# Side products of the band stages move from the rounds to the places in front of rounds one and two, into two banks, with VectorE as their copier

## The chip, the cores and the metric

The kernel runs on one core of one Trainium2 chip. The metric is the device time of one execution in microseconds (us), the median of three timed runs. Engines: TensorE (PE in the rows; its weight loads PEld), VectorE (DVE), ScalarE (ACT), GpSimd (POOL) and SyncE (SP, whose queue issues DMA).

## The reference

Two layers on x of 4 sequences of 512 positions with 128 features, each an attention part and a part with experts. The first layer's attention is the one at stake: each position t looks at a window of the 64 positions that end with it, in 16 heads.

```python
disp = (x @ W_disp).reshape(B, T, nh, bd).transpose(0, 2, 1, 3)       # 16 heads of 16
val = (x @ W_val).reshape(B, T, nh, hs).transpose(0, 2, 1, 3)         # 16 heads of 8
strain = disp_win - disp[:, :, :, None, :]                            # 64 neighbours of each t
bond_act = gelu(strain @ W_strain + rel_emb @ W_pos)
bond_logits = (bond_act @ W_bond)[..., 0]
damage_act = gelu(strain @ W_dmg + b_dmg)
damage = sigmoid((damage_act @ W_dmg_out)[..., 0] + b_dmg_out[0])
logits = where(cmask, bond_logits - 10.0 * damage, -inf)
weights = softmax(logits, axis=-1)
out = einsum('bntd,bntde->bnte', weights, val_win)                    # then @ W_cproj
```

The first layer's experts (16, four chosen for each position, with gate weights `route`) are added beside it: `acc = acc + r[..., None] * y`, and y holds a bias row of each expert, so that the biases together are the product of `route` with the 16 bias rows. The second layer is another attention and eight experts of which two are chosen.

## The kernel before, in words

Each engine has a program of its own, written out by hand, and signals (semaphores) tie them together. Between the stages all engines meet at a barrier.

The windowed attention is done for two groups of eight heads, `g` = 0 and 1. For each group there is first a long loop over the 64 neighbours, which leaves the logits in `Z`, and then a *band stage*, the one that the change touches. Stage one (g = 0) and stage two (g = 1) run the same code:

- TensorE's `weigh(k)` transposes the logits of one quarter (128 positions) into PSUM, VectorE takes the maximum and subtracts it (L832, L836), ScalarE takes the exponential (L872), four times.
- SyncE writes each quarter's weights to a DRAM tensor `band`, and SyncE and GpSimd read them back skewed into `wide` (L799), so that the windows become bands of a matrix. TensorE's first wait for such rows is `d_band_in0`.
- Then come four *rounds*, k = 0 to 3 (round one to four below). `turn(k)` transposes the round's 32 blocks in eight groups of four (L958) into four PSUM banks in turn. ScalarE copies the even groups to `wtT` (L898), VectorE the odd ones (L844), and a group waits until the copy of the group four before it is done. `values(k)` makes the value products of a round (L945), ScalarE copies them (L889). `gather(k)` forms denominators (L976) and numerators (L984) in the bank `summed(k)`, which is `WB[:, 3]` or `ZT[:, 8:12]` in turn, and VectorE's `divide(k)` takes the reciprocal and multiplies (L849, L851).
- `side(i)`, i = 0 to 7, stands twice in each round: behind `turn(k)` and behind `gather(k)`. It has nothing to do with the bands. In stage one side(i) is one product for the next loop: a part of `AD` for the group g = 1, L928, copied by ScalarE (L878). In stage two the sides with even i are four transposes of `route` (L935), copied by ScalarE to 16 partitions of `w1T` (L881), and the odd ones the four products with the experts' bias rows (L937), which VectorE adds to `ACC` (L856). All of them use the bank `WB[:, 2]`, so each waits until the one before is copied.

Behind stage one the next loop starts, behind stage two the second layer (L1177 is its first product). A stage ends when its last engine is done.

## Time and profile before

| | us |
|---|---|
| median of three timed runs | 1243.27 |
| lowest, highest | 1239.11, 1246.47 |
| profiled execution | 1248.83 |
| its span | 1247.1 |
| TensorE busy (share of the span) | 1033.0 (83%) |
| VectorE busy | 966.8 (78%) |
| ScalarE busy | 822.9 (66%) |
| GpSimd busy | 165.9 (13%) |

The span runs from the first to the last instruction; the time of the execution is a little longer. Busy shares are means over the whole program. A matmul of fp32 operands stands as two records in the profile and a transpose as one, each with a weight load of its own.

### The profile page before, as it was taken

What the parts mean: (1) busy time and instruction counts of PE and PEld (TensorE: products, weight loads), DVE (VectorE), ACT (ScalarE), POOL (GpSimd) and SP (SyncE); (2) the same over time, 40 slices, a digit from 0 to 9 for tenths busy, and PEclk for the clock granted to TensorE, in tenths of its full rate; (3) what the DMA queues carried; (4) which work ended last, traced back from release to release, by engine and by line L of the source; (5) the groups of instructions that cost most, each with busy time, mean ns of one, the idle gap of its engine ahead of it and who ended that gap; (6) DMA issues with size and microseconds to landing.
All of it is one profiled execution on the core that took longest, in us unless ns stands there. A gap on an engine that the chain in (4) does not pass through costs nothing. (4 is left out here: it accounts for less than half of the span.)

```text
span 1247.1 us, 23038 instructions
## 1 busy us (share of the span) xinstructions
PE 1033.0 (83%) x9629; PEld 533.1 (43%) x9629; DVE 966.8 (78%) x1221; ACT 822.9 (66%) x886; POOL 165.9 (13%) x257
## 2 busy tenths in 40 slices
PE   1679899998848499888899759898669999989887
PEld 1323333333447333333333358733315565556532
DVE  6699999999763799999999734558767467576746
ACT  0779999999762589999999652243146646565564
POOL 4100000000140100000000320313740000000072
PEclk9889999999979799999999968688569989989988
DMA  7310000000075200000000093000123423432221
GB/s 249 113 23 1 2 1 1 2 1 2 1 198 139 52 2 1 2 2 1 1 1 2 1 278 61 21 1 1 58 77 87 117 85 102 127 89 81 79 60 40
DMA packets 71750, 67.39 MB, mean 54 GB/s; under 512 B 6148, under 2 KB 63200, under 8 KB 71648
## 3 DMA queue, kind: packets, MB, share of 16 engines
q1 hardware_dynamic: 67808, 55.51, 15.8%
q0 software_dynamic: 3840, 10.43, 3.2%
q8 instruction: 76, 1.25, 0.4%
q14 instruction: 26, 0.21, 0.1%
HBM read 41.80 MB, written 20.97 MB: 50 GB/s over the span
## 5 line engine op out<-in xcount | busy, mean ns | idle before, releaser
L538 DVE SCALAR_TENSOR_TENSOR ring<-AD,PT 128x1808 f32<-128x1808 f32 (+15 forms) x128 | 284.0, 2219 | 4.0 <-POOLq L520 3.2
L683 PE MATMUL LG<-ring,lred 128*32 128x456 f32 (+15 forms) x2048 | 232.0, 572 | 1.3 <-ACT ring L635 1.3
L1841 DVE TENSOR_REDUCE MX<-SS 128x2 f32<-128x1024 f32 x128 | 155.6, 1219 | 67.0 <-PE SS L1583 66.7
L1771 ACT ACTIVATE EX<-SS 128x1024 f32<-128x1024 f32 x128 | 131.1, 1028 | 111.0 <-PE SS L1583 110.2
L625 ACT ACTIVATE ring<-ring 128x3616 f32<-128x3616 f32 (+15 forms) x50 | 169.9, 3398 | 3.7 <-DVE ring L538 3.7
L705 PE MATMUL SD<-DS,eyes 96*32 96x456 bf16 (+15 forms) x2496 | 156.7, 370 | 9.5 <-ACT ring L630 7.4
L633 ACT ACTIVATE ring<-ring 128x1824 f32<-128x1824 f32 (+15 forms) x78 | 141.0, 1807 | 0.0
L705 PEld LDWEIGHTS SD<-DS,eyes 96*32 96x32 bf16 x2496 | 57.8, 96 | 152.9 <-ACT ring L630 57.6
L538 DVE SCALAR_TENSOR_TENSOR ring<-AD,bdmg 128x1808 f32<-128x1808 f32 (+15 forms) x50 | 110.6, 2212 | 0.0
L718 PE MATMUL PY<-w2T,xg 128*128 128x128 f32 x512 | 74.1, 288 | 35.3 <-DVE xg L563 35.3
L683 PEld LDWEIGHTS LG<-ring,lred 128*32 128x32 f32 x2048 | 59.3, 110 | 99.3 <-issue 76.9
L1583 PE MATMUL SS<-KS,QS 32*128 32x512 f32 x256 | 72.5, 562 | 34.9 <-DVE MX L1841 32.3
L712 PE MATMUL PH<-tT,w1s 128*128 128x512 f32 x128 | 73.6, 658 | 30.3 <-DVE xg L558 23.4
L630 ACT ACTIVATE ring<-SD,bdmg 128x912 f32<-128x912 f32 (+15 forms) x78 | 82.8, 1062 | 22.2 <-PE SD L705 20.3
L718 PEld LDWEIGHTS PY<-w2T,xg 128*128 128x128 f32 x512 | 61.9, 191 | 70.0 <-DVE xg L563 55.5
L635 ACT ACTIVATE ring<-SD,bdmg 128x912 f32<-128x912 f32 (+15 forms) x78 | 82.6, 1059 | 1.4 <-PE SD L705 0.6
L570 DVE SCALAR_TENSOR_TENSOR ACC<-PY,route,ACC 128x128 f32<-128x128 f32 x256 | 71.6, 341 | 9.4 <-PE PY L718 9.4
L1603 PE MATMUL PW<-EX,VA 128*32 128x512 f32 x512 | 75.5, 668 | 0.1
L525 POOL COPY w1s<-w1T 128x128 f32<-128x128 f32 x16 | 12.6, 788 | 461.6 <-PE PH L712 461.6
L1583 PE MATMUL SS<-QS,KS 32*128 32x512 f32 x256 | 69.5, 543 | 5.3 <-ACT EX L1771 2.7
L1748 ACT ACTIVATE HB<-PHh,b1c 128x128 f32<-128x128 f32 x156 | 44.5, 368 | 31.0 <-PE PHh L1535 30.4
L1583 PEld LDWEIGHTS SS<-KS,QS 32*128 32x128 f32 x256 | 26.9, 204 | 85.4 <-DVE MX L1841 57.6
(338 smaller groups left out, 1500.8 us busy)
## 6 DMA issues: line engine op xcount, KB each, us to landing
w1s<-in_L_ffn_W SPq DMA_DIRECT2D x39, 256.0 KB, 3.0
w2s<-in_L_ffn_W SPq DMA_DIRECT2D x39, 256.0 KB, 3.0
band<-zs SPq DMA_DIRECT2D x8, 1024.0 KB, 8.8
wide<-band POOLq DMA_DIRECT2D x16, 380.0 KB, 8.9
wide<-band SPq DMA_DIRECT2D x16, 380.0 KB, 11.0
band<-Z SPq DMA_DIRECT2D x4, 1024.0 KB, 8.9
xs<-Z SPq DMA_DIRECT2D x4, 640.0 KB, 8.8
xl<-xs SPq DMA_DIRECT2D x10, 256.0 KB, 2.9
```

The lines of the kernel that those rows point to most:

```text
L538: return v.scalar_tensor_tensor(out=ring[:, slot, s, :, t0:T], in0=AD[:, s, :, j + t0:j + T], scalar=extra, in1=AD[:, s, :, PAD + t0:PAD + T],
L625: act.activation(tiles, tiles, ACT.Gelu).then_inc(gelu_done, 1)
L630: act.activation(ring[:, slot, 1, 0:2, t0:T], SD[:, :, t0:T], ACT.Gelu, bias=bdmg[:, 0:1]).then_inc(sd_taken, 1)
L633: act.activation(tiles, tiles, ACT.Gelu)
L635: act.activation(ring[:, slot, 1, 2:4, t0:T], SD[:, :, t0:T], ACT.Gelu, bias=bdmg[:, 0:1]).then_inc(gelu_done, 1)
L683: mm = pe.matmul(LG[32 * b:32 * b + 32, par, s, t0:T], lred[:, s, n % 4, :], ring[:, slot, s, b, t0:T], start=(n % 4 == 0), stop=(n % 4 == 3))
L705: mm = pe.matmul(SD[32 * q:32 * q + 32, i, t0:T], eyes[0:96, sign, :], DS[0:96, q, 2 * half + i, at:at + T - t0], start=(sign == 0), stop= ...
L718: mm = pe.matmul(PY[:, i, :], xg[:, c % 2, P * i:P * i + P], w2T[:, bass.ds(HG * g + it, 1), :].rearrange("p o c -> p (o c)"), start=True, ...
L1583: mm = pe.matmul(bank[:, n, :], rows[r:r + 32, b % 2, q, P * t:P * t + P], cols[r:r + 32, b % 2, q, :], start=True, stop=True)
L1603: mm = pe.matmul(PN[32 * hh:32 * hh + 32, :], VA[:, b % 2, t, 4 * q + hh, :], EX[:, q % 2, hh, t, :], start=(t == 0), stop=(t == NT - 1))
L1771: act.activation(EX[:, Q % 2, hh:hh + 2, t, :], SS[:, slot, :, :], ACT.Exp, scale=SCALE1).then_inc(freed[slot], 1)
L1841: v.tensor_reduce(MX[:, t, p // 2, hh:hh + 2], SS[:, slot, :, :], AX.X, ALU.max).then_inc(freed[slot], 1)
```

## The change

The four PSUM banks of transposes and the bank `WB[:, 3]` stay as they are. The side products now use `WB[:, 2]` and `ZT[:, 8:12]` in turn, and VectorE takes all of them out. They no longer stand in each round but at two places: five (stage one) or six (stage two) behind the four `weigh` and the first `values`, in front of round one, and three or two in front of round two. `gather(1)`, which sums into `ZT[:, 8:12]`, waits until all sides are copied. In stage two their order is other: two sets of transposes of `route`, then the two sets of products that use them, and so on, each to its own place in `w1T`.

TensorE in stage one, before, from the first value products (L945) over round one to the first transposes of round two. `wad` is the weight of a side product, `wide` the rows read back, `lones` and `vp` the operands of the sums:

```order
-L945 MATMUL ZT<-wval,xnT 128x64 x8
-L958 MATMUL WB<-ident,wide 128x128 x8
-L958 MATMUL ZT<-ident,wide 128x128 x8
-L958 MATMUL WB<-ident,wide 128x128 x8
-L958 MATMUL ZT<-ident,wide 128x128 x8
-L928 MATMUL WB<-xnT,wad 128x512
-L945 MATMUL ZT<-wval,xnT 128x64 x8
-L976 MATMUL WB<-wtT,lones 32x128 x32
-L984 MATMUL WB<-wtT,vp 32x64 x64
-L928 MATMUL WB<-xnT,wad 128x512
```

and now, where L956 are the values, L937 a side product, L969 the transposes of `wide`, L991 and L999 the sums:

```order
+L956 MATMUL ZT<-wval,xnT 128x64 x8
+L937 MATMUL WB<-xnT,wad 128x512
+L937 MATMUL ZT<-xnT,wad 128x512
+L937 MATMUL WB<-xnT,wad 128x512
+L937 MATMUL ZT<-xnT,wad 128x512
+L937 MATMUL WB<-xnT,wad 128x512
+L969 MATMUL WB<-ident,wide 128x128 x8
+L969 MATMUL ZT<-ident,wide 128x128 x8
+L969 MATMUL WB<-ident,wide 128x128 x8
+L969 MATMUL ZT<-ident,wide 128x128 x8
+L956 MATMUL ZT<-wval,xnT 128x64 x8
+L991 MATMUL WB<-wtT,lones 32x128 x32
```

One side product stood behind round one's transposes and one behind its sums. Now five stand in front of the transposes, and three more behind the sums, in front of the next round's transposes.

TensorE in stage two, before, the same place; L935 are transposes of `route`, L937 the products with the bias rows `b2r`:

```order
-L945 MATMUL ZT<-wval,xnT 128x64 x8
-L958 MATMUL WB<-ident,wide 128x128 x8
-L958 MATMUL ZT<-ident,wide 128x128 x8
-L958 MATMUL WB<-ident,wide 128x128 x8
-L958 MATMUL ZT<-ident,wide 128x128 x8
-L935 MATMUL WB<-ident,route 16x128 x4
-L945 MATMUL ZT<-wval,xnT 128x64 x8
-L976 MATMUL WB<-wtT,lones 32x128 x32
-L984 MATMUL WB<-wtT,vp 32x64 x64
-L937 MATMUL WB<-b2r,w1T 128x128 x4
```

and now, from behind the value products; L948 are the transposes of `route`, L946 the products:

```order
+L948 MATMUL WB<-ident,route 16x128 x4
+L948 MATMUL ZT<-ident,route 16x128 x4
+L946 MATMUL WB<-b2r,w1T 128x128 x4
+L946 MATMUL ZT<-b2r,w1T 128x128 x4
+L948 MATMUL WB<-ident,route 16x128 x4
+L948 MATMUL ZT<-ident,route 16x128 x4
+L969 MATMUL WB<-ident,wide 128x128 x8
+L969 MATMUL ZT<-ident,wide 128x128 x8
+L969 MATMUL WB<-ident,wide 128x128 x8
+L969 MATMUL ZT<-ident,wide 128x128 x8
+L956 MATMUL ZT<-wval,xnT 128x64 x8
+L991 MATMUL WB<-wtT,lones 32x128 x32
```

Four sets of transposes and two of products stand in front of round one.

VectorE in stage one, before, from the division behind round one (L849, L851) through its copies of round two (L844):

```order
-L849 RECIPROCAL Z<-WB 128x256
-L851 TENSOR_TENSOR attT<-WB,Z 128x2x128
-L844 COPY wtT<-WB 128x512
-L844 COPY wtT<-ZT 128x512
-L844 COPY wtT<-WB 128x512
-L844 COPY wtT<-ZT 128x512
```

and now, where L855 and L857 are the division, L863 the copy of a side product and L850 the copies of transposes:

```order
+L855 RECIPROCAL Z<-WB 128x256
+L857 TENSOR_TENSOR attT<-WB,Z 128x2x128
+L863 COPY AD<-ZT 128x512
+L863 COPY AD<-WB 128x512
+L863 COPY AD<-ZT 128x512
+L850 COPY wtT<-WB 128x512
+L850 COPY wtT<-ZT 128x512
+L850 COPY wtT<-WB 128x512
+L850 COPY wtT<-ZT 128x512
```

Three copies of side products stand between the division and the copies of round two.

```diff
--- before.py
+++ after.py
@@ -763,7 +763,7 @@
         with ExitStack() as sm:
             vp = sb(f"vp{g}", [P, 2, 8, HG, 32], F32, sm)
             zs = sb(f"zs{g}", [P, 2, NG, WIN, 4], F32, sm)
-            rtT = w1T[0:E0, 0:NT, :]
+            SIDES = ([0, 1, 2, 3, 4], [5, 6, 7]) if g < G - 1 else ([0, 1, 2, 3, 4, 5], [6, 7])
             wide = sb(f"wide{g}", [P, WIDE, NG, P, 4], F32, sm)
             wtT = sb(f"wtT{g}", [P, 32, P], F32, sm)
             diffs = [wtT[:, 16 * n:16 * n + 16, :].rearrange("p a t -> p (a t)").rearrange("p (n q j) -> p n q j", n=32, j=4) for n in range(2)]
@@ -783,6 +783,12 @@
 
             def turned(i):
                 return banks[i % 4]
+
+            def side_bank(i):
+                return ZT[:, 8:12, :] if i % 2 else WB[:, 2]
+
+            def pair_of(i):
+                return 2 * (i // 4) + i % 2, i % 4 >= 2
 
             def summed(k):
                 return ZT[:, 8:12, :] if k % 2 else WB[:, 3]
@@ -850,18 +856,30 @@
                     v.wait_ge(rc_ready, m + 1)
                     v.tensor_tensor(attT[:, g, :, P * ti:P * ti + P], summed(k)[:, 2:4, :], rc, ALU.mult).then_inc(att_ready, 1)
 
-                def bias(i):
-                    v.wait_ge(side_pe, 2 * i + 2)
-                    a = ACC[:, NT * i:NT * i + NT, :]
-                    v.tensor_tensor(a, a, WB[:, 2], ALU.add).then_inc(side_sb, 1)
+                def side(i):
+                    bank = side_bank(i)
+                    if g < G - 1:
+                        v.wait_ge(ad_pe, 8 + i + 1)
+                        v.tensor_copy(AD[:, i // 4, i % 4, PAD:PAD + T], bank.rearrange("p n t -> p (n t)")).then_inc(ad_sb, 1)
+                        return
+                    p, product = pair_of(i)
+                    v.wait_ge(side_pe, i + 1)
+                    if product:
+                        a = ACC[:, NT * p:NT * p + NT, :]
+                        v.tensor_tensor(a, a, bank, ALU.add).then_inc(side_sb, 1)
+                    else:
+                        v.tensor_copy(w1T[0:E0, NT * p:NT * p + NT, :], bank[0:E0]).then_inc(side_sb, 1)
 
                 for k in range(NT):
                     weigh(k)
+                for i in SIDES[0]:
+                    side(i)
                 for k in range(NT):
+                    if k == 1:
+                        for i in SIDES[1]:
+                            side(i)
                     turn(k)
                     divide(k)
-                    if g == G - 1:
-                        bias(k)
 
             @block.scalar
             def _(act):
@@ -871,14 +889,6 @@
                         act.wait_ge(d_out[k - 2], 16 * (g + 1))
                     act.activation(zs[:, k % 2].rearrange("p g s n -> p g n s"), diffs[k % 2].rearrange("p (g n) q j -> p g n (q j)", n=4), ACT.Exp
                                    ).then_inc(ex_ready, 1)
-
-                def side(i):
-                    if g < G - 1:
-                        act.wait_ge(ad_pe, 8 + i + 1)
-                        act.copy(AD[:, i // 4, i % 4, PAD:PAD + T], WB[:, 2].rearrange("p n t -> p (n t)")).then_inc(ad_sb, 1)
-                    elif i % 2 == 0:
-                        act.wait_ge(side_pe, i + 1)
-                        act.copy(rtT, WB[0:E0, 2]).then_inc(side_sb, 1)
 
                 def values(k):
                     m, par = M0 + k, k % 2
@@ -905,10 +915,8 @@
                 values(0)
                 for k in range(NT):
                     turn(k)
-                    side(2 * k)
                     if k + 1 < NT:
                         values(k + 1)
-                    side(2 * k + 1)
 
             @block.tensor
             def _(pe):
@@ -923,18 +931,21 @@
                     mm.then_inc(zt_ready, 1)
 
                 def side(i):
+                    bank = side_bank(i)
                     if g < G - 1:
-                        pe.wait_ge(ad_sb, 8 + i)
-                        pe.matmul(WB[:, 2].rearrange("p n t -> p (n t)"), wad[:, 1, i // 4, :], xnT[:, i % 4, PAD:PAD + T],
+                        pe.wait_ge(ad_sb, 8 + max(i - 1, 0))
+                        pe.matmul(bank.rearrange("p n t -> p (n t)"), wad[:, 1, i // 4, :], xnT[:, i % 4, PAD:PAD + T],
                                   start=True, stop=True).then_inc(ad_pe, 1)
                         return
-                    pe.wait_ge(side_sb, i)
+                    p, product = pair_of(i)
+                    if i >= 2:
+                        pe.wait_ge(side_sb, i - 1)
                     for n in range(NT):
-                        t = NT * (i // 2) + n
-                        if i % 2 == 0:
-                            mm = pe.transpose(WB[0:E0, 2, n, :], route[:, t, :], ident[:])
+                        t = NT * p + n
+                        if product:
+                            mm = pe.matmul(bank[:, n, :], w1T[0:E0, t, :], b2r[:], start=True, stop=True)
                         else:
-                            mm = pe.matmul(WB[:, 2, n, :], rtT[:, n, :], b2r[:], start=True, stop=True)
+                            mm = pe.transpose(bank[0:E0, n, :], route[:, t, :], ident[:])
                     mm.then_inc(side_pe, 1)
 
                 def values(k):
@@ -965,6 +976,10 @@
                     pe.wait_ge(vw_sb, m + 1)
                     if k >= 2:
                         pe.wait_ge(att_ready, m - 1)
+                    if k == 1 and g < G - 1:
+                        pe.wait_ge(ad_sb, 16)
+                    if k == 1 and g == G - 1:
+                        pe.wait_ge(side_sb, 8)
                     acc = summed(k)
 
 
@@ -991,13 +1006,16 @@
                 pe.wait_ge(zs_ready, M0 + 3)
                 values(0)
                 pe.wait_ge(zs_ready, M0 + NT)
+                for i in SIDES[0]:
+                    side(i)
                 for k in range(NT):
+                    if k == 1:
+                        for i in SIDES[1]:
+                            side(i)
                     turn(k)
-                    side(2 * k)
                     if k + 1 < NT:
                         values(k + 1)
                     gather(k)
-                    side(2 * k + 1)
 
 
 def second_layer(nc, t_in, out, l1, sb, psum, sem, ident, ACC, nhalf, stats, mv, rstd, carried):
```

## Rows read from the trace of the kernel before

**Rows 1.** Timeline of TensorE, stage one: start us, us, engine line operation tile, count, idle before

```profile
366.56 1.96 PE L958 MATMUL WB<-ident,wide 128*128 128x128 f32 x8 [9.67 <-DMA wide<-band]
...
371.96 1.02 PE L928 MATMUL WB<-xnT,wad 128*128 128x512 f32 x2
372.83 1.89 PE L945 MATMUL ZT<-wval,xnT 128*128 128x64 f32 x16
...
380.47 1.49 PE L984 MATMUL WB<-wtT,vp 128*32 128x64 f32 x44 [2.65 <-issue]
381.89 2.03 PE L928 MATMUL WB<-xnT,wad 128*128 128x512 f32 x2
383.76 1.12 PE L958 MATMUL WB<-ident,wide 128*128 128x128 f32 x8
...
387.60 1.02 PE L928 MATMUL WB<-xnT,wad 128*128 128x512 f32 x2
...
394.09 0.69 PE L984 MATMUL ZT<-wtT,vp 128*32 128x64 f32 x33 [0.52 <-issue]
394.71 1.13 PE L928 MATMUL WB<-xnT,wad 128*128 128x512 f32 x2
395.68 1.12 PE L958 MATMUL WB<-ident,wide 128*128 128x128 f32 x8
...
411.76 1.02 PE L928 MATMUL WB<-xnT,wad 128*128 128x512 f32 x2
412.75 1.95 PE L976 MATMUL ZT<-wtT,lones 128*32 128x128 f32 x64
```

**Rows 2.** Timeline of TensorE through stage two, the same columns.

```profile
732.76 1.96 PE L958 MATMUL WB<-ident,wide 128*128 128x128 f32 x8 [7.40 <-DMA wide<-band]
...
739.67 1.90 PE L945 MATMUL ZT<-wval,xnT 128*128 128x64 f32 x16
...
749.03 0.65 PE L984 MATMUL WB<-wtT,vp 128*32 128x64 f32 x14 [3.92 <-issue]
749.60 2.07 PE L937 MATMUL WB<-b2r,w1T 16*128 16x128 f32 x8
751.60 1.98 PE L958 MATMUL WB<-ident,wide 128*128 128x128 f32 x8
...
757.31 0.60 PE L935 MATMUL WB<-ident,route 128*16 128x128 f32 x4
757.75 1.90 PE L945 MATMUL ZT<-wval,xnT 128*128 128x64 f32 x16
...
764.25 1.15 PE L937 MATMUL WB<-b2r,w1T 16*128 16x128 f32 x8
765.33 1.53 PE L958 MATMUL WB<-ident,wide 128*128 128x128 f32 x8
...
770.75 0.60 PE L935 MATMUL WB<-ident,route 128*16 128x128 f32 x4
```

**Rows 3.** Timeline of VectorE through stage one, the same columns.

```profile
356.92 2.29 DVE L836 TENSOR_TENSOR wtT<-WB,mx 128x2048 f32<-128x2048 f32 x1
368.62 0.69 DVE L844 COPY wtT<-WB 128x512 f32<-128x512 f32 x1 [9.41 <-PE WB L958]
...
396.95 0.68 DVE L844 COPY wtT<-WB 128x512 f32<-128x512 f32 x1
```

**Rows 4.** Timeline of VectorE through stage two, the same columns.

```profile
723.86 2.29 DVE L836 TENSOR_TENSOR wtT<-WB,mx 128x2048 f32<-128x2048 f32 x1
...
789.23 0.42 DVE L851 TENSOR_TENSOR attT<-ZT,Z 128x256 f32<-128x256 f32 x1
789.57 0.68 DVE L856 TENSOR_TENSOR ACC<-ACC,WB 128x512 f32<-128x512 f32 x1
```

**Rows 5.** Stretches of stage one: busy us by engine, granted clock, DMA share, GB/s.

```profile
356.90:366.50 9.60, 0.00 (x0) 0.00 (x0) 2.29 (x1) 6.11 (x6) 1.16 (x2) 0.50 1.05 257
...
377.80:380.47 2.67, 0.02 (x2) 0.00 (x1) 0.00 (x0) 0.00 (x0) 0.00 (x0) 0.98 1.05 263
```

## The prediction

> **What bounds the bands now.** Read first the page's slices, to find the two band stages as the places where DMA is busy in the middle of the span, then the timeline of TensorE through the first of them [rows 1]. In each stage TensorE transposes scores, stands still for the first rows that DMA brings back, and then works without a stop through four rounds of transposes (L958), values (L945), and sums (L976, L984), with a side product (L928 in the first stage, L935 and L937 in the second) twice in each round. What the reader is to see: an idle of 9.67 us before 366.56, with DMA as its releaser, and after it almost no idle that another engine causes. Where TensorE stops, it is inside L984 and the releaser reads "issue": 2.65 us in the first round, 0.52 in the second. So in the rounds the side products lie on the path, while the long wait in front of them is empty. In the second stage it is the same: 7.40 us empty before 732.76, and 3.92 us of issue in the first round [rows 2]. VectorE is free from 359.21 (356.92 + 2.29) in stage one and from 726.15 (723.86 + 2.29) in stage two [rows 3, 4]; TensorE's first wait also asks for that last subtraction, so this is when the moved products can start.
>
> The profiled execution took 1248.83 us, 1.73 more than its span and 5.56 above the median of the three timed runs, 1243.27. The sum is made in the profile's own time, and the difference is taken off the median.
>
> **Stage one, step by step.** (a) Five products move into the wait. One costs 1.87 us while the granted clock is 0.50, that is 1.2 GHz (381.89 to 383.76), and 0.87 at 2.4 GHz (371.96 to 372.83) [rows 1]. From 359.21 there are 7.35 us until the rows land at 366.56. The clock stood at 0.50 all through the empty wait [rows 5]. How soon it rises can be read from the transposes: they took 5.40 us in round one (366.56 to 371.96) and 3.84 in round two (383.76 to 387.60), and as work at half clock takes twice as long, 3.1 of the 5.40 us were at half clock. If it rises 3.1 us into the new work too, the five need 3.1 us (1.7 products) + 3.3 × 0.87 = 6.0 us and end at 365.2, inside the wait. The latest rise in the rows is in stage two: 5.71 us of transposes from 751.60 had 3.7 us at half clock, so until 755.3, 6.3 us after TensorE resumed at 749.03 [rows 2]. With that the five end at 366.9, 0.4 late. VectorE's copy of 128x512 from a bank takes 0.69 us [rows 3]; with two banks it fits beside the product after it, so it adds nothing.
>
> (b) The first round then starts with a clock that is already up. Its transposes cost 3.84 us instead of 5.40. And product 0 is gone from behind them: 0.87. Together −2.43 us.
>
> (c) The issue stall. Before, it comes after 84 of L984's 128 records in round one (the row after it holds 44) and after 95 in round two (33 are left) [rows 1]. A round has 488 matmul and weight-load instructions, and 11 more records, each with its weight load, make 22 more: close to 512 from stall to stall. So the stall belongs to a place in TensorE's code, with a fetch behind it, and it is long while the band's transfers fill the DMA engines: the 2.65 us had a DMA share of 1.05 [rows 5]. I take it that its fetch is asked for when TensorE reaches some place before, so it moves forward with TensorE and keeps its length. The price if it does not is a rival below. The Trainium skill, "Runtime: NRT & Kernel Launch", Instruction fetch mechanics, has blocks of 256 instructions that each sequencer fetches itself, and says that this is mostly hidden. The block agrees with the spacing of the stalls, the hiding does not: the rows have 2.65 and 3.92 us. By its word alone the gain of (b) would be kept whole.
>
> (d) Before the second round three products now stand where one stood. Before: 1.87 us, 381.89 to 383.76. After: the third writes the bank of the first and waits for its copy, which VectorE makes only behind the division of the first sums. In round three that chain is in the rows: the sums end at 394.71, and VectorE's first copy behind the division starts at 396.95 and ends at 397.63: 2.92 us behind the sums, call it 3.0 with the signal [rows 1, 3]. Plus 0.9 for the third product makes 3.9, so +2.0. The rows of the second round are there by then: TensorE found them at 383.76 without a wait, and by (b) and (d) it comes at nearly the same time, 383.3.
>
> (e) The products behind the transposes of rounds two and three go: 2 × 0.87 = −1.74. The one in round four gives nothing: the sums there start 0.99 us after the product does (411.76 to 412.75), about what VectorE's last copy takes, and the sums wait for that copy too.
>
> (f) The products in front of rounds three and four go, at 0.97 each (394.71 to 395.68). But now the transposes start at once, and the sixth group of four writes the bank that VectorE empties only behind its division, 3.0 us after the sums. TensorE is there after 5 × 0.48 = 2.4 us. So 0.6 is given back: −0.37 each, −0.74. The last product stood behind the last sums beside VectorE's division, which ends the stage: nothing.
>
> Stage one: −2.43 + 2.0 − 1.74 − 0.74 = −2.9 us.
>
> **Stage two.** (a, b) Four sets of transposes and two sets of products move into 726.15 to 732.76, 6.6 us. A set of transposes costs 0.44 at the full clock (757.31 to 757.75), a set of products 1.08 (764.25 to 765.33) or 2.00 (749.60 to 751.60) [rows 2]. At half clock all the way that is 4 × 0.9 + 2 × 2.0 = 7.6, and 1.0 late; with a rise 3.1 us in, about 5.8 with the waits for VectorE's copies. I take 0.3 late. The first round was at half clock for most of its transposes: 732.76 to 739.67 with its set of transposes, 6.91 us. It becomes 3.84 + 0.3: −2.8. (d) Two sets of products before round two instead of one; no bank is shared with an unemptied one, so it is TensorE's time: 2 × 2.0 against 2.0, while round two's transposes, half cold before (751.60 to 757.31 with 5.71), now catch more of the risen clock, about 4.4. From the sums' end to the end of the transposes 8.4 against 7.71: +0.7. With an early rise it is 6.9, −0.8. (e) Transposes of route in rounds two and three: −0.88. (f) Products before rounds three and four: 1.08 − 0.6 each, −0.95. Behind the last multiply (789.23 + 0.42) VectorE added the last product until 790.25 [rows 4]; that add is gone and the stage ends on the multiply, at 789.65: −0.6. Stage two: −2.8 + 0.7 − 0.88 − 0.95 − 0.6 = −4.5 us.
>
> ScalarE's copies go to VectorE, which stands idle in the wait for 9.41 us before its first copy [rows 3]. ScalarE is not waited for in the rounds except by signals that come sooner now. The loops behind each stage find the same data and start earlier by what is saved. Both stages: −7.4 us, so 1241.4 in the profile's time and 1243.27 − 7.4 = 1235.9, say 1236.0, in the measured.
>
> **Rivals.** 1. The clock does not rise in the wait. Then five products take 9.35 us and end at 368.6, 2.0 late, and the transposes keep their 5.40: stage one loses 3.6 of its gain; stage two starts 1.0 late instead of 0.3 and keeps 6.47 us of transposes: another 3.3. Result −0.5: 1242.8. For it: the work in stage two's wait has gaps for the copies. Against: in stage one TensorE has nothing to wait for.
>
> 2. The stall of the first round ends when it did, since the fetch lies behind the band's transfers, whose time the change does not touch. Then (b) is swallowed in both stages, 2.4 and 2.8, and −2.2 is left: 1241.1. For it: the stall is long only under full DMA. Against: it stands at a place of the code, and the fetch of a later place comes off faster transposes.
>
> 3. Slower: the side products kept TensorE's array full between the sums of one round and the transposes of the next; without them the clock falls in the rounds more often. The trace has the half rate once without a long stop: behind the product at 764.25, round three of stage two took 5.42 us (765.33 to 770.75) instead of 3.84, 1.6 more. With such a fall in each of the other five rounds behind the first ones, 8 us go and the kernel stands at 1236.0 + 8 = 1244.0; with falls as long as in round one of stage two (6.47 us of transposes instead of 3.84) 13 us, and 1249. It decides from 15 us more at 1.2 GHz than before, as half of that time is lost. The Trainium skill, "TensorE: Matmul & The Clock Gate", A second HAM failure mode: psum-queue depth-cycling, says that many short idles between groups bring the clock up and down; the new 0.6 us stops of (f) would be such. Against: round three of stage one came behind a stop of 0.52 us, and its product 0.6 us later was at the full clock (0.97) [rows 1].
>
> 4. More gain: the clock comes early in (d) of both stages and stays up in round three of stage two: −1.5 − 1.6 on top, 1232.9.
>
> **Chances.** The forecast holds 0.55, its own range 1232 to 1240; rival 1 0.09, rival 2 0.16, rival 3 0.12, rival 4 0.08. A measurement of this kernel tells 0.5%, 6.2 us, from no change, so the bound lies at 1237.1, close under the forecast. Of the forecast some 0.68 lies under it, with rival 4 that is 0.45 faster. Slower by over 0.5%, above 1249.5, needs the upper part of rival 3 together with some of 1 or 2, or longer falls than it counts: 0.07. The same: all the rest, 0.48. The range, 1230.5 to 1245.0, takes in rivals 1, 2 and 4 and the near end of 3.
>
> **What would show it.** Right: five products in front of the first rows of stage one with no idle over 1 us before them, first transposes of 3.8 us, and the issue stall again in L984, nearer to its start (8 records in stage one: 16 more instructions stand before it) and about 2.5 us earlier; before round two an idle of some 0.3 to 1.3 us with VectorE's copy as releaser; in rounds three and four one of about 0.6 before the sixth group. Wrong: first transposes over 5 us (1), the stall ending near 380.5 and 749.0 (2), rows of transposes of over 5 us in the later rounds (3), or a wait for DMA before round two.

## The result and the profile after

| | before | changed |
|---|---|---|
| median of 20 runs, us | 1241.47 | 1237.91 |
| lowest, highest | 1236.47, 1248.27 | 1234.45, 1243.55 |
| ratio | | 0.9962 (0.9946 to 0.9977) |
| profiled execution, its span | 1248.83, 1247.1 | 1234.47, 1232.6 |
| stage one, stage two | 79.7, 84.3 | 77.2, 78.1 |

The change makes the kernel faster by 0.38%, 4.7 us by the ratio, with 2.9 to 6.7 us as the interval. The forecast was 7.3 us; the two medians differ by 3.6. That 1237.91 stands only 1.9 us from the forecast's 1236.0 is in part luck: the forecast started from 1243.27, the median of three runs, and over 20 runs the kernel before is at 1241.47. A stage is counted from the start of VectorE's first addition in it to the end of its last multiply or add. By the two profiles alone the stages would have gained 8.7 us, and by the spans 14.5; both say more than the 20 runs, and the experiments ask why.

The busy times in the page of the changed kernel:

```profile
PE 1029.9 (84%) x9629; PEld 527.6 (43%) x9629; DVE 974.9 (79%) x1233; ACT 816.3 (66%) x874; POOL 165.4 (13%) x257
```

TensorE through stage one of the changed kernel (timeline: start us, us, engine, line, operation, tile, count, idle before). L937 is a side product, L969 the transposes, L956 the values, L991 and L999 the sums:

```profile
358.65 2.07 PE L937 MATMUL WB<-xnT,wad 128*128 128x512 f32 x2 [2.26 <-DVE wtT L842]
...
364.19 1.13 PE L937 MATMUL WB<-xnT,wad 128*128 128x512 f32 x2
365.85 1.23 PE L969 MATMUL WB<-ident,wide 128*128 128x128 f32 x8 [0.53 <-DMA wide<-band]
...
369.80 1.90 PE L956 MATMUL ZT<-wval,xnT 128*128 128x64 f32 x16
...
373.40 1.28 PE L999 MATMUL WB<-wtT,vp 128*32 128x64 f32 x75
378.37 0.98 PE L999 MATMUL WB<-wtT,vp 128*32 128x64 f32 x53 [3.69 <-issue]
379.28 1.79 PE L937 MATMUL ZT<-xnT,wad 128*128 128x512 f32 x2
380.86 1.91 PE L937 MATMUL WB<-xnT,wad 128*128 128x512 f32 x2
382.57 1.25 PE L937 MATMUL ZT<-xnT,wad 128*128 128x512 f32 x2
383.66 1.12 PE L969 MATMUL WB<-ident,wide 128*128 128x128 f32 x8
...
387.49 1.90 PE L956 MATMUL ZT<-wval,xnT 128*128 128x64 f32 x16
...
392.77 0.86 PE L999 MATMUL ZT<-wtT,vp 128*32 128x64 f32 x44 [0.28 <-issue]
...
396.55 0.75 PE L969 MATMUL WB<-ident,wide 128*128 128x128 f32 x4 [0.31 <-DVE wtT L850]
...
409.61 1.96 PE L991 MATMUL ZT<-wtT,lones 128*32 128x128 f32 x64 [0.83 <-ACT wtT L908]
```

Where 9.67 us stood empty [rows 1] there are five products, 358.65 to about 365.3, and then 0.53 us of wait for the rows. Round one starts at the full clock and reaches the values 3.95 us later (365.85 to 369.80), where it took 6.27 before with its product. The issue stall came after 75 records instead of 84 and lasted 3.69 us instead of 2.65. Before round two stand three products for 4.38 us (379.28 to 383.66), against 1.87. At 396.55 is the new wait for VectorE's copy: the transposes of four that end at 396.24 wait 0.31 us.

VectorE in the same stage:

```profile
365.36 0.69 DVE L863 COPY AD<-WB 128x512 f32<-128x512 f32 x1 [0.29 <-PE WB L937]
...
379.40 1.76 DVE L855 RECIPROCAL Z<-WB 128x256 f32<-128x256 f32 x1 [8.71 <-PE WB L999]
...
381.53 0.68 DVE L863 COPY AD<-ZT 128x512 f32<-128x512 f32 x1
```

The last of the five copies in the wait is over at 366.05, long before VectorE is wanted for the transposes. The division starts at 379.40, and the copy behind it at 381.53, as [rows 3] had it for round three.

TensorE through stage two (L948 transposes of `route`, L946 products with the bias rows):

```profile
723.19 1.02 PE L948 MATMUL WB<-ident,route 128*16 128x128 f32 x4 [2.53 <-DVE wtT L842]
...
729.56 1.02 PE L948 MATMUL ZT<-ident,route 128*16 128x128 f32 x4
730.38 1.91 PE L969 MATMUL WB<-ident,wide 128*128 128x128 f32 x8
...
736.06 1.90 PE L956 MATMUL ZT<-wval,xnT 128*128 128x64 f32 x16
...
743.73 0.86 PE L999 MATMUL WB<-wtT,vp 128*32 128x64 f32 x43 [2.68 <-issue]
744.52 1.82 PE L946 MATMUL WB<-b2r,w1T 16*128 16x128 f32 x8
...
747.98 1.98 PE L969 MATMUL WB<-ident,wide 128*128 128x128 f32 x8
...
753.47 1.90 PE L956 MATMUL ZT<-wval,xnT 128*128 128x64 f32 x16
...
761.97 0.75 PE L969 MATMUL WB<-ident,wide 128*128 128x128 f32 x4 [0.34 <-DVE wtT L850]
```

The same stretch in the view of windows (length, then busy us of PE, PEld, DVE, ACT, POOL, granted clock, DMA share, GB/s):

```profile
723.19:730.38 7.19, 7.19 (x33) 5.38 (x34) 3.35 (x5) 4.46 (x5) 1.16 (x2) 0.50 1.07 275
```

The six sets fill 723.19 to 730.38, 7.19 us, with no idle of TensorE that the profile shows, and all of it at half clock (granted 0.50): a set of transposes still costs 0.82 us at its end. Round one starts at half clock too and takes 5.68 us to the values (6.91 in [rows 2]). Before round two the two sets and the transposes take 8.95 us (744.52 to 753.47).

### The profile page after: what moved, and what is told of

Same layout as the page of the kernel before. It is cut to its first block and busy times, and to the rows that moved or that the text cites. A ratio compares the mean times of both kernels' runs of the same rounds, so it can differ in the third digit from the quotient of the medians.

```text
span 1232.6 us, 23040 instructions
## 1 busy us (share of the span) xinstructions
PE 1029.9 (84%) x9629; PEld 527.6 (43%) x9629; DVE 974.9 (79%) x1233; ACT 816.3 (66%) x874; POOL 165.4 (13%) x257
## 3 DMA queue, kind: packets, MB, share of 16 engines
q8 instruction: 76, 1.25, 0.4%
```

## The experiments

The kernels ran in three groups of four, each group on one chip beside the kernel before, whose medians were 1279.3, 1279.7 and 1242.5 us. The second layer took 484 to 495 us in the profiles of the first two groups and 451 to 459 in the others, while the first layer outside the stages took the same everywhere, within 1.5 us. So ratios are read within a group, and stage lengths and cut kernels across them: the five kernels without the second layer spend 631.4 to 633.2 us outside the two stages, whichever chip they ran on.

### The same two kernels again

Edit: none.

> The kernel before once more, for a second profile. Measured gain over 20 runs each is about 4.7 us (ratio 0.9962), while the two profiles differ by 8.8 us inside the two band stages and by 14.5 us in the span. Theory A (the first profile of before had bad luck in the clock and the issue stall of stage two): this profile has stage one near 79.8 us (matrix transposes' start to the last multiply), stage two shorter than the first profile's 84.3, 80 to 83 us. Theory B (the bands gain 8.8 us and something behind them gives 4 us back): stage two is 84.3 again, and the parts outside the bands are 4 us shorter here than in the changed kernel.

> The changed kernel once more. Ratio 0.996 again. Theory A: stage one 77.2 us, stage two 78 to 80, and the parts outside the bands vary by several us in either direction with no sign of the change. Theory B: the parts outside the bands are 4 us longer than in the kernel before.

Measured: ratio 0.9971 (0.9943 to 0.9999) for the kernel before against itself, 0.9961 (0.9941 to 0.9982) for the changed one. The latter is the main result once more; the former shows that a ratio of one group can be off by 0.3%, nearly as much as the 0.38% at stake. Stages 82.7 and 81.7 before, 78.0 and 78.7 changed. The parts outside the stages: 1083.1 and 1116.9 before, 1077.3 and 1120.7 changed, so the sign of the difference turns from one pair to the other. Stage two of before was 84.3 in the first profile and 81.7 here, as Theory A had it; stage one was 3 us longer here, which it had not.

### Without the second layer

```diff
-            second_layer(nc, t_in, out, l1, sb, psum, sem, ident, ACC, nhalf, stats, mv, rstd, carried)
+            copied = sem("copied")
+            block = l1.enter_context(nc.Block())
+
+            @block.sync
+            def _(sp):
+                sp.dma_start(out.rearrange("b t c -> (b t) c").rearrange("(n p) c -> p n c", p=P), ACC[:]).then_inc(copied, 16)
+                sp.wait_ge(copied, 16)
```

> The kernel before with the whole second layer left out; the first layer's sum goes to the output as it is. What is left ends just behind stage two, so its time tells the band stages without the 455 to 490 us behind them, which differ by several us from one profile to the next. About 795 us. It is to be compared with the same cut of the changed kernel. Theory A (the second layer hides nothing; in most runs the bands gain only 5 us): the two cuts differ by 4 to 6 us. Theory B (the bands gain 8 us in every run, and some 3 us are given back behind them): they differ by 8 us.

> The changed kernel with the whole second layer left out. Theory A: 4 to 6 us under the cut kernel before. Theory B: 8 us under it. The forecast's own sum says 7.4.

Measured: medians 793.42 (792.54 to 797.35) and 789.65 (787.75 to 790.36), five runs each: 3.8 us. Their profiles have stages of 79.3 and 80.2 us before, 77.3 and 79.1 changed, 3.1 us less, and 632.2 and 631.8 us outside them. The 3.8 us are just under the 4 to 6 of Theory A and far from the 8 of Theory B: the stages themselves gain about 4 us here, and nothing behind them needs to give anything back. Over the three profiles of each, the two stages together are 164.0, 164.4 and 159.5 us before, and 155.3, 156.7 and 156.4 changed. The kernel before is the one that varies, and the forecast was made from one of its long executions.

### The clock alone

```diff
                 pe.wait_ge(zs_ready, M0 + NT)
+                for i in range(5):
+                    pe.matmul(WB[:, 2].rearrange("p n t -> p (n t)"), wad[:, 1, i // 4, :], xnT[:, i % 4, PAD:PAD + T],
+                              start=True, stop=True)
```

> The kernel before, with five more products of 128x512 into the free bank in TensorE's wait for the first rows, in both stages, whose results nobody reads; the side products stay in the rounds. It shows what the clock alone gives. By the forecast's step (b): first transposes of 3.84 us instead of 5.40 and 6.47 us, so 1.6 + 2.6 = 4.2 us less, and no more, ratio 0.997. If instead the clock is not what shortened round one, nothing changes, ratio 1.000. If the issue stall takes the gain back by ending where it did, the transposes are short but the sums of round one end no earlier: ratio 0.999 or 1.000.

Measured: ratio 0.9994 (0.9970 to 1.0017), no change that can be told; the interval still holds the 0.997. The stages took 80.2 and 80.9 us. TensorE at the start of round one in stage two (L995 are the five products, L958 the transposes, L935 side product 0):

```profile
727.14 6.95 PE L995 MATMUL WB<-xnT,wad 128*128 128x512 f32 x10 [2.53 <-DVE wtT L836]
733.92 1.11 PE L958 MATMUL WB<-ident,wide 128*128 128x128 f32 x8
...
737.75 0.60 PE L935 MATMUL WB<-ident,route 128*16 128x128 f32 x4
```

and its windows:

```profile
727.14:733.92 6.78, 6.78 (x10) 2.94 (x11) 0.00 (x0) 4.46 (x5) 1.16 (x2) 0.64 1.06 276
```

The transposes take 3.83 us. So five products of 128x512 in stage two's wait do bring the clock up, in 6.8 us, which the changed kernel's six sets do not in 7.2 us. In stage one the transposes took 3.95 as well. The issue stalls behind them were 2.76 and 3.76 us. The gain of round one is there: its sums end 40.9 us behind the start of stage one (42.9, 45.6 and 42.8 in the three profiles of before) and 41.4 behind that of stage two (43.7, 43.5, 42.1). Later rounds of stage one took some of it back, with stalls of 1.57 us in round two and 0.86 in round four, where before had 0.22 to 0.52 and none.

### One bank

```diff
             def side_bank(i):
-                return ZT[:, 8:12, :] if i % 2 else WB[:, 2]
+                return WB[:, 2]
-                        pe.wait_ge(ad_sb, 8 + max(i - 1, 0))
+                        pe.wait_ge(ad_sb, 8 + i)
```

The wait of stage two is changed in the same way.

> The changed kernel, but with all side products in the one bank of the kernel before, so that each waits until VectorE has copied the one ahead. If the second bank is what lets them fit into the wait: about 0.9 us more for each product or set in the wait, so the transposes of round one start 2 to 3 us late in stage one and 4 to 6 us late in stage two, with visible waits of TensorE for the copies, and the kernel is 6 us slower than the changed one: ratio 1.000 against before. If one bank is enough (the copies lie in slack): ratio 0.996.

Measured: ratio 1.0103 (1.0071 to 1.0135), 18 us over the changed kernel's 0.9961, three times the expected. Stages 88.8 and 84.9 us. TensorE in stage one:

```profile
358.97 2.07 PE L937 MATMUL WB<-xnT,wad 128*128 128x512 f32 x2 [2.44 <-DVE wtT L842]
361.83 2.08 PE L937 MATMUL WB<-xnT,wad 128*128 128x512 f32 x2 [0.78 <-DVE AD L863]
...
370.40 2.08 PE L937 MATMUL WB<-xnT,wad 128*128 128x512 f32 x2 [0.78 <-DVE AD L863]
372.27 1.56 PE L969 MATMUL WB<-ident,wide 128*128 128x128 f32 x8
...
376.56 1.90 PE L956 MATMUL ZT<-wval,xnT 128*128 128x64 f32 x16
```

Each product but the first waits 0.78 us for a copy, as expected, but each also takes 1.87 us: with these stops the clock never rises, for 13.3 us (358.97 to 372.27, granted 0.50). Round one starts 6 us late. The second bank gives more than the stops it removes; it gives the clock.

### Holding the later reads back

```diff
             def read(engine, k, half):
+                if k >= 2:
+                    engine.wait_ge(nd_pe, M0 + 1)
```

> The changed kernel, with the reads of rounds three and four held back until the sums of round one are done. Theory C (the issue stall inside the first sums is a fetch of code that queues behind the band's transfers): the stall of 3.69 and 2.68 us in the first sums shrinks to about 0.5 in both stages, as in the later rounds, and the rows of round three, asked for at about 376 instead of 372 us, still land by 388, before the 391 at which TensorE would ask: 5 us less than the changed kernel, ratio 0.992 against before. Theory D (the stall belongs to that code and not to the load): it stays near 3 us and moves nothing: ratio 0.996. If the held rows are late, a wait for DMA stands before round three or four.

Measured: ratio 0.9988 (0.9965 to 1.0010); both theories' ratios fail. The two issue stalls of stage one, in the sums of rounds one and two:

```profile
378.43 1.71 PE L1001 MATMUL WB<-wtT,vp 128*32 128x64 f32 x53 [3.46 <-issue]
...
396.14 1.49 PE L1001 MATMUL ZT<-wtT,vp 128*32 128x64 f32 x44 [3.29 <-issue]
```

and the stretches around them (busy us of PE, PEld, DVE, ACT, POOL, then granted clock, DMA share, GB/s):

```profile
370.00:373.00 3.00, 3.00 (x59) 2.93 (x61) 0.71 (x2) 1.17 (x5) 0.00 (x0) 1.00 1.09 271
...
388.00:392.80 4.80, 4.80 (x165) 4.62 (x163) 0.69 (x1) 0.94 (x5) 0.00 (x0) 1.00 1.05 280
```

The stall of round one stayed, 3.46 us: at 370 to 373 the DMA engines were still full with the earlier transfers. But the stall of round two, 0.17 to 0.52 us in the three profiles of the changed kernel, grew to 3.29 us, and in stage two from none to 3.75, where the held transfers now ran beside it. No wait for DMA rows came up. So the stall follows the load of the DMA engines shortly before it. What was wrong in Theory C was when that load counts.

### Free places instead of the front of round two

```diff
-            SIDES = ([0, 1, 2, 3, 4], [5, 6, 7]) if g < G - 1 else ([0, 1, 2, 3, 4, 5], [6, 7])
+            SIDES = ([0, 1, 2, 3, 4], [5]) if g < G - 1 else ([0, 1, 2, 3, 4, 5], [])
...
                     if k + 1 < NT:
                         values(k + 1)
+                    else:
+                        side(6)
                     gather(k)
+                side(7)
```

The banks, the waits and the copying engines of the moved products follow.

> The changed kernel with less in front of round two: there only product 5 (stage one) or nothing (stage two). The others go to two places which the rows of before show as free: between round four's transposes and its sums, where TensorE waits 0.83 us for the last copies, and behind the last sums, beside VectorE's division; ScalarE copies the two of stage one, VectorE adds the two of stage two. If the three and two products in front of round two cost what the trace shows (4.4 and 3.5 us, at half clock), this saves 2.8 us in stage one less about 0.8 for transposes that now meet the low clock, and 3.5 in stage two less 1.5 for the same and 0.8 for the last add: some 3 us under the changed kernel, ratio 0.9935. If the low clock takes all of it (the clock rises at the same time, whatever is done until then): 1 us, ratio 0.995.

> The kernel with the two free places (one or no side product in front of round two), without the second layer. In its full form round two's front got 3 us shorter in stage one, but the issue stall in the sums of round two grew from 0.2 to 0.5 us up to 3.6 us, since they now run while the transfers still do. So it should be only 0 to 2 us under the cut changed kernel (789.65): 788 to 789.5. If it is 3 us or more under it, the longer stall was chance.

Measured: ratio 0.9954 (0.9933 to 0.9974), not to be told from the changed kernel's; the cut form 788.05 us (786.82 to 789.61), 1.6 us under the cut changed kernel, inside what was expected. TensorE in stage one of the full form (L945 a side product, L977 transposes, L964 values, L1007 sums):

```profile
378.62 0.98 PE L1007 MATMUL WB<-wtT,vp 128*32 128x64 f32 x53 [3.58 <-issue]
379.53 1.13 PE L945 MATMUL ZT<-xnT,wad 128*128 128x512 f32 x2
...
384.65 1.90 PE L964 MATMUL ZT<-wval,xnT 128*128 128x64 f32 x16
...
393.26 0.77 PE L1007 MATMUL ZT<-wtT,vp 128*32 128x64 f32 x40 [3.59 <-issue]
```

From the sums to the next values it is 5.12 us (379.53 to 384.65) instead of 8.21. That gain came, and the sums of round two handed it back: an issue stall of 3.59 us, and 2.15 in the cut form. The trace's DMA records show why. The packet that brings TensorE's code for this place (see the last section) began at 390.38, though TensorE came to the place that asks for it some 2.7 us earlier than in the changed kernel (an estimate from the records' counts); there it began at 390.06, 390.56 and 390.13 in the three profiles.

### Moving the boundary of the code blocks

```diff
                 values(0)
+                if g == 0:
+                    for n in range(30):
+                        pe.matmul(ZT[0:32, 0, 0:8], ident[0:32, 0:32], ident[0:32, 0:8], start=True, stop=True)
                 pe.wait_ge(zs_ready, M0 + NT)
```

> The changed kernel without its second layer, and with 30 tiny products (8 columns, read by nobody, 120 instructions with their weight loads) between the first values and the side products of stage one. They shift the code behind them by 120 instructions. Theory E (TensorE asks for the next block of its code on crossing a block's boundary, 256 instructions ahead; the stall in the sums comes because both boundaries lie in the 384 quick instructions of the sums, and lasts as the fetch takes 5 to 6 us under the band's transfers): the boundary now falls where the 256 instructions before it take 6 us or more, so the stalls of 3.3 us in both stages' first sums vanish or stay under 1 us. The tiny products cost 1 us or less in the wait of stage one. Total 4 to 6 us less than the cut changed kernel (789.65): 784 to 786. Theory F (the stall has to do with the load and this code, not with the place of a boundary): stalls of 3 us as before, 790.

> The same with the 30 tiny products of the padded kernel in stage one. Theory E: the stalls of rounds one and two vanish in both stages (boundaries at about instruction 160, 190 and 220 of the 384 of the sums), so that now the shorter front of round two counts: 3 + 2.6 us from round one and 3.6 + 1.6 us from round two, 8 to 10 us under the cut kernel with free places, 779 to 781. Theory F: no change.

> The same with its second layer, and with 34 more tiny products behind the last sums of stage two, so that the second layer's code stands to the block boundaries as before. If Theory E holds in the cut kernels: 12 to 15 us under the kernel before, ratio 0.989 to 0.991. If the second layer gives some back, 0.993.

Measured: 782.02 us (780.54 to 786.26) for the cut changed kernel with the 30 tiny products, against 789.65 without: 7.6 us less, for 120 instructions more. The stages are 73.1 and 75.1 us. TensorE in its stage one (L1016 the tiny products, L975 transposes, L1005 sums, L943 side products):

```profile
357.00 3.37 PE L1016 MATMUL ZT<-ident 32*32 32x8 f32 x60
...
366.57 1.23 PE L975 MATMUL WB<-ident,wide 128*128 128x128 f32 x8
...
374.11 1.97 PE L1005 MATMUL WB<-wtT,vp 128*32 128x64 f32 x128
376.01 1.13 PE L943 MATMUL ZT<-xnT,wad 128*128 128x512 f32 x2
...
379.02 1.13 PE L943 MATMUL ZT<-xnT,wad 128*128 128x512 f32 x2 [1.02 <-DVE AD L869]
379.98 1.11 PE L975 MATMUL WB<-ident,wide 128*128 128x128 f32 x8
...
387.41 1.97 PE L1005 MATMUL ZT<-wtT,vp 128*32 128x64 f32 x128
```

The sums of rounds one and two run through all 128 records with no stall. The two kernels ran on different chips, but outside the stages they take 631.8 and 632.1 us; so the 8.2 us by which their stages differ (156.4 and 148.2, one profile each) come from the change. The tiny products cost 3.3 us and delay the first side product by 0.8 us, counted from the stage's start, yet round one starts at the same time. And with no stall the clock stays up, so the side products before round two take 0.97 us each, and the third waits 1.02 us for VectorE's copy: only now does the wait of the forecast's step (d) show. In stage two the sums of rounds one and two have no stall either, but the stall did not vanish altogether. The next boundary fell into round two's transposes (L975), and the clock fell behind it (granted 0.64 from 742.20 to 747.00):

```profile
742.07 1.60 PE L975 MATMUL ZT<-ident,wide 128*128 128x128 f32 x7 [1.73 <-issue]
```

Theory E holds against Theory F, and the gain is more than it foresaw (4 to 6 us): with no stall in the sums of round one the half clock behind it is gone too, so that the stretch from the values to the end of these sums is 4.3 and 4.2 us shorter in the two stages.

The kernel with free places did not follow: 786.86 us (786.23 to 789.43) with the tiny products against 788.05 without, 1.2 us where 8 to 10 were expected. Its stage one took 72.4 us, although a stall of 1.63 us stands in the transposes of round two (at 380.52), but stage two took 79.1:

```profile
735.28 1.97 PE L1013 MATMUL WB<-wtT,vp 128*32 128x64 f32 x128
...
742.20 1.38 PE L983 MATMUL ZT<-ident,wide 128*128 128x128 f32 x7 [1.15 <-issue]
743.37 3.51 PE L970 MATMUL ZT<-wval,xnT 128*128 128x64 f32 x16
...
752.95 2.50 PE L1013 MATMUL ZT<-wtT,vp 128*32 128x64 f32 x88 [2.25 <-issue]
```

The sums of round one have no stall (735.28), but the next boundary falls into the transposes of round two with 1.15 us, the clock falls there (the values' row has 3.51 us instead of 1.90), and the block after it is late as well, 2.25 us. Its full form, with 34 more tiny products at the end of stage two: ratio 0.9941 (0.9918 to 0.9965), 7.3 us where 12 to 15 were expected, median 1233.90 against 1242.45. It is the lowest ratio of the full kernels, but its interval overlaps the changed kernel's. The changed kernel with the 30 tiny products was not run with its second layer, so its 7.6 us are shown for the cut kernel alone.

## Why the forecast was right in kind and too large in size

The mechanism was right: the waits take the work, the rounds lose it, the front of round two pays for part. Stage one came out close to the sum at each step. Stage two did not. The table has the means of the three profiles of each kernel (full, full again, cut), in us; the forecast's steps beside them.

| stretch | stage one: before, changed | forecast | stage two: before, changed | forecast |
|---|---|---|---|---|
| stage start to round one | 27.90, 27.49 | 0 | 26.86, 27.40 | +0.3 |
| round one to its values | 6.38, 3.88 | −2.43 | 6.25, 5.10 | −3.1 |
| values to end of first sums | 9.42, 9.83 | 0 | 9.90, 9.24 | 0 |
| sums to the values of round two | 6.97, 7.93 | +1.1 | 7.79, 9.37 | +0.3 |
| to the values of round three | 11.78, 10.66 | −1.24 | 12.33, 10.10 | −0.92 |
| to the last sums | 12.10, 11.71 | −0.37 | 12.33, 11.40 | −0.48 |
| the last add or copy behind the last multiply | 0, 0 | 0 | 0.6, 0 | −0.6 |
| the whole stage | 80.6, 77.5 | −2.9 | 82.1, 78.6 | −4.5 |

**The steps that failed are (a, b) and (d) of stage two.** The forecast let the clock rise 3.1 us into the moved work, a figure read from the full transposes of round one. The sets of stage two are transposes of 16 columns and products of 16 rows. The profile shows no idle of TensorE in the 7.19 us that they take, so the gaps that the forecast's rival 1 named are not there, and the granted clock stayed at 0.50; it rose only 2 to 4 us into round one. The row for (b) and (a) together is −0.6 us in the means instead of −2.8. The clock-alone run shows that it was the kind of work and not the stage: there the same wait, filled with five products of 128x512, ended at the full clock. The forecast also took 6.91 us as the cost of round one before, the longest of three (6.91, 6.34, 5.50). Step (d) was priced with a rise some 5 us behind the sums (4.0 for the products and 1.1 into the transposes); in the changed kernel the transposes' lengths put it 7 to 8 us behind them, so this stretch took 9.4 us instead of 7.8, +1.6 where +0.3 was forecast.

What made up for part of it was not forecast: the short stalls in the sums of rounds two and three of stage two (0.71, 0.32, 0.53 and 0.59, 0.44, 0.40 us before) are nearly gone (0.21 once in three profiles), which fits the boundaries of the code blocks that the moved products shifted, though no run tests it by itself; and the fall of the clock that cost round three 1.6 us in [rows 2] was in one of three profiles. That the fall counted as a loss of before in the measured span of the first profile, though the sum had not used it, is part of why the two profiles show 8.7 us where the means show 6.5.

**Step (d) of stage one was right in sum, wrong in cause.** It priced +2.0 by VectorE's division. In the first profile of the changed kernel the three products ran at half clock nearly throughout, 4.38 us, and did not wait; in the other two the first product alone was that slow, 3.95 us in all, with a wait for the copy of 0.19 us. The division's wait came out only where the stall was gone, 1.02 us in the padded kernel.

**Step (c) held on the average only.** The stall moved with the code: 75 records instead of 84 (nine fewer, where the forecast had eight), and 85 instead of 114. It did not keep its length: 2.65, 3.79, 2.58 us before and 3.69, 3.69, 3.30 changed in stage one, 3.92, 4.18, 3.56 and 2.68, 3.12, 3.29 in stage two. The sums over both stages are 6.9 and 6.6 us in the means. So rival 2 is refuted as it was put: the stall's end moved forward by 2.5 us in the means of stage one (from 42.3 to 39.8 us behind the stage's start) and by 1.9 in those of stage two (from 42.4 to 40.5). But what it feared is real in the kernel with free places, where an earlier arrival was paid to a longer stall.

**(e) and (f) were right,** with 0.31 us of wait at the sixth group instead of 0.6, and 0.83 us at the sums of round four, where nothing was to be had. Rival 3 had no run for it: no profile of the changed kernel has a fallen clock in rounds three and four. Rival 1 is half true, in stage two.

What stays open: the means of three profiles say 6.5 us, the 20 runs 4.7 (2.9 to 6.7), the cut kernels 3.8. All agree within their spread, but the share of before's long executions (stages of 164 against 159.5 us) cannot be told from three. Whether the padded changed kernel keeps its 7.6 us with the second layer behind it is open too.

## What to carry to other kernels

Work moved into an engine's wait is paid twice if it also brings the clock up, but only if it is work that does: here 128x512 products back to back did, and neither small transposes with products of 16 rows, busy for 7.19 us, nor 128x512 products with stops of 0.78 us did. Where a row reads "issue" in a run of many quick instructions, count the instructions between such rows; if the spacing is constant, look for the code packets in the DMA records. The place of the boundary can be worth more than the reordering (7.6 us against 3.8 in the kernels without the second layer), and a reordering changes it unseen. Take a step's price from more than one profile where the clock is in it.

## What the runs showed of the hardware that was not expected

**TensorE's code comes in packets that the trace records.** The DMA view has a queue of its own for them. These are its lines for the cut changed kernel and for the same with 120 more TensorE instructions (kind, packets, MB, share of the 16 engines):

```profile
q8 instruction: 58, 0.95, 0.5%
...
q8 instruction: 59, 0.97, 0.5%
```

The full kernels have 76 packets, 1.25 MB, for 19,258 matmul and weight-load instructions and some 340 signals, so that one packet of 16 KB holds about 256 instructions. Counted through TensorE's program, signals included, the issue stalls in the sums stand 511 to 513 instructions apart from one round to the next, in every kernel without tiny products.

**A block is asked for one block ahead, and it is the start of the packet that comes late.** Where TensorE was 256 instructions before a stall is an estimate from the records' counts, as is the time at which it was there. The packets' times are those of the DMA records:

| stall | 256 instructions before, us | packet begins, ends | TensorE goes on |
|---|---|---|---|
| before, stage one, round two; DMA share 0.06 | 391.2 | 391.69, 392.57 | 394.09 |
| before, stage one, round one | 375.2 | 378.01, 379.19 | 380.47 |
| changed, stage one, round one | 371.9 | 375.90, 376.94 | 378.37 |
| before, stage two, round one | 742.9 | 746.42, 747.65 | 749.03 |
| later reads held back, stage one, round two | 390.2 | 393.71, 394.72 | 396.14 |
| free places and tiny products, stage two, round two | 742.20 | 750.24, 751.58 | 752.95 |

The packet itself takes 0.9 to 1.3 us, and TensorE goes on 1.3 to 1.5 us behind its end, in every row. What differs is the time until it begins: 0.5 us where the DMA engines were idle, 2.8 to 4.0 where the band's transfers filled them, and 8.0 once. From the asking to the end of the stall that is about 3 us idle and 5.3 to 6.5 under load. In the last row the DMA share was 1.03 up to 750.20 and 0.18 behind it, so the packet began as the transfers ran out. Why it waited that long is open: the cut changed kernel with tiny products passed the same boundary at 742.07, and its packet began at 745.13.

**Where a boundary hides.** The sums' 384 instructions take 3.7 us without a stall (1.77 for L997 before 374.11, and on to 376.01), so two boundaries inside them show whenever the fetch takes 5 us. Two boundaries with transposes and values between them, some 6 us of work, hid it in stage one of the padded kernel and left 1.73 us of it in stage two. Moving the boundary by 120 instructions took 3.30 and 3.29 us of stall out of the first sums, and 0.9 to 1.0 us of half clock behind each.
